# Token rows kept in one buffer of twelve from load to store, second operand copies, and a new order of steps, in a four-layer attention kernel

## What is computed

```python
# L0, and L3 with other weights: cross attention to ctx, residual
Q = x @ Wq + bq;  K = ctx @ Wk + bk;  V = ctx @ Wv + bv
x = x + softmax(Q @ K.T / 16) @ V @ Wo + bo
# L1: layer norms, attention to ctx ("a") and to side ("v"), then a layer norm and a dense layer ("fc")
t = attend_a(ln(x), ln(ctx)) + attend_v(ln(x), ln(side)) + x
x = ln(t) @ fc_W + fc_b + t
# L2: attention whose softmax runs over the query axis, layer norm with gain and bias
w = softmax((x @ Wq + bq) @ (ctx @ Wk + bk).T / 16, over x's tokens)
x = ln(w @ (ctx @ Wv + bv) + x) * gamma + beta
```

## Time and profile before

| | us |
|---|---|
| median of 3 runs | 557.83 |
| lowest and highest run | 557.55, 558.46 |
| span of the profiled execution, first to last instruction | 557.1 |
| PE busy | 545.8 (98%) |
| DVE busy | 478.4 (86%) |
| POOL busy | 480.7 (86%) |
| ACT busy | 447.2 (80%) |
| transfers of q1, share of 16 engines | 43.0% |

### The profile page before, as it was taken

One profiled execution on the slowest core, in us unless ns is written; L12 is line 12 of the kernel. 1 busy time (PEld: TensorE's weight loads), 2 busy tenths in 40 slices (PEclk: granted clock), 3 DMA queues, 4 the chain that ended last, 5 costly groups with the idle time before them and its releaser, 6 DMA issues.

```text
span 557.1 us, 16210 instructions
## 1 busy us (share of the span) xinstructions
PE 545.8 (98%) x4492; PEld 534.9 (96%) x4492; DVE 478.4 (86%) x1472; ACT 447.2 (80%) x1568; POOL 480.7 (86%) x672
## 2 busy tenths in 40 slices
PE   8999999999999999999999999999999999999995
PEld 7999999999999999989999999999999999999994
DVE  2588799888999889989897997999898987998884
ACT  2799987889778797869879798877888979798663
POOL 4999997999988989979997899977999998766793
PEclk9999999999999999999999999999999999999999
DMA  8993472344553345453247263453433432221112
GB/s 238 352 326 126 118 215 90 121 147 149 172 168 111 113 143 152 149 174 124 80 139 202 67 190 102 145 172 122 139 122 115 124 105 78 77 96 58 39 40 95
DMA packets 74440, 76.58 MB, mean 137 GB/s; under 512 B 7664, under 2 KB 58224, under 8 KB 74352
## 3 DMA queue, kind: packets, MB, share of 16 engines
q1 hardware_dynamic: 74352, 75.55, 43.0%
HBM read 50.87 MB, written 24.64 MB: 136 GB/s over the span
## 4 chain that ended last, share of the span: by engine, by line
PE 87%; POOL 4%; DMA 3%; issue 2%; DVE 2%; SPq 1%; ACT 1%; DVEq 0%; POOLq 0%; ACTq 0%
PE bank L793 15%; PE bank L806 10%; PE bank L800 9%; PE bank L776 7%; PE bank L817 5%; PE bank L819 5%; PE bank L818 5%; PE bank L949 5%; PE bank L927 5%; PE bank L784 5%; PE bank L830 4%; PE bank L902 3%; PE bank L903 3%; PE bank L904 3%; DMA side_in<-in_side 1%
## 5 line engine op out<-in xcount | busy, mean ns | idle before, releaser
L1065 ACT ACTIVATE prob_L<-bank,neg_max_L 128x128 f32<-128x128 f32 x320 | 114.5, 375 | 15.7 <-DVE neg_max_L L1376 13.6
L1065 ACT ACTIVATION_READ_ACCUMULATOR prob_L<-bank,neg_max_L 128x1 f32 x320 | 68.3, 214 | 0.0
L1376 DVE TENSOR_REDUCE neg_max_L<-bank 128x2 f32<-128x256 f32 (+1 forms) x128 | 60.5, 479 | 7.1 <-PE bank L800 4.3
L1546 POOL TENSOR_TENSOR rstd_ln<-var_eps_ln,minus_half 128x2 f32<-128x2 f32 x64 | 45.2, 707 | 18.5 <-ACT var_eps_ln L1078 18.2
L994 ACT ACTIVATE oT_hi_L<-bank 128x256 fp32r<-128x256 f32 (+1 forms) x96 | 44.4, 471 | 12.4 <-PE bank L806 11.1
L1219 DVE TENSOR_TENSOR oT_lo_L<-bank,oT_hi_L 128x256 fp32r<-128x256 f32 (+1 forms) x96 | 47.2, 501 | 5.6 <-ACT oT_hi_L L994 4.9
L994 ACT ACTIVATE probT_L<-bank 128x256 f32<-128x256 f32 (+1 forms) x96 | 44.4, 470 | 9.0 <-PE bank L784 8.6
L1333 DVE BATCH_NORM_STATS2 stats_ln<-x 128x6 f32<-128x256 f32 x128 | 47.5, 413 | 0.2
L1219 DVE TENSOR_TENSOR xT_lo_L<-bank,xT_hi_L 128x512 fp32r<-128x512 f32 x64 | 43.1, 677 | 3.7 <-ACT xT_hi_L L994 3.5
L1611 POOL TENSOR_TENSOR x_bias<-x,bias_fc 128x512 f32<-128x512 f32 x32 | 41.1, 1285 | 5.8 <-DVE x L1409 5.8
L1588 POOL TENSOR_TENSOR xT_lo_L<-x_in,xT_hi_L 128x512 fp32r<-128x512 f32 x32 | 41.2, 1286 | 5.4 <-ACT xT_hi_L L994 5.4
...
## 6 DMA issues: line engine op xcount, KB each, us to landing
...
keysT<-keys_out SPq DMA_DIRECT2D x128, 64.0 KB, 2.0
...
```

What stands on the lines that cost most here:

```text
L1065: last = activation(at(prob[k], g)[:, b, :], block(bank, b), ACT.Exp, bias=at(neg_max[k], g)[:, b:b + 1], accum_out=at(total[k], g)[:, b:b ...
L1376: dve.tensor_reduce(at(neg_max[k], g)[:], scores, AX.X, ALU.max, negate=True).then_inc(done[f"max_{k}"], 1)
L1546: pool.tensor_tensor(at(rstd[k], g)[:], at(var_eps[k], g)[:], minus_half[:, 0:n], ALU.pow).then_inc(done[f"rstd_{k}"], 1)
```

## The change

- The eleven kinds of row buffers are replaced by one, `x`, with 12 copies. load_x fills it, and every step of POOL and DVE named above reads and writes it in place until `store` sends it. The transposed half of the input goes into a buffer of its own, `xT_in` (3 copies), by an issue of its own, `load_xT`. `xhat` (2) remains for the norm of L1.
- Waits follow from that. load_x of group g waits for x_bias of g-4 and from group 12 on for the landing of the store of g-12. store waits for the store of g-4, load_ctx for hi_ctx of g-4. On POOL, x1_bias waits for norm_ln1 (it waited for out_L0), x2_bias for T_fc and stats_lnf (it waited for out_L1), x_res for T_L3 besides norm_ln2. On DVE, out_L2 waits for turn_x3. The waits for free copies of x1, x2, x3, x4, y and the biases fall away.
- Copies that go from 1 to 2: xT_hi and xT_lo of L1, fc and L3, qT_L1, oT_hi and oT_lo of L1 and L3, prob_L2, keys_turned, x3_turned. x3T goes from 2 to 3. ctx_in (10), side_in (3), keys (3), B2 (6), V2 (3) and the others stay.
- STARTS, PREPARATIONS and SEATS are new for every step. At the start SP's order is now cols, x of groups 0 to 3, ctx 0, xT 0, ctx 1, side 0 and 1, the weights Wq and Wk of L0, those of L2, xT 1, ctx 2, xT 2, side 2, the L2 value weights, ctx 3, xT 3, side 3, fc, send_keys 0, ctx 4, Wq and Wk of L1v, Wv and Wo of L0, side 4. It was cols, the Wq and Wk of L2, side 0, ctx 0, Wv and Wo of L0, Wq and Wk of L1v, two rows, x 0, Wq and Wk of L0. A weight pair Wq, Wk is 384 KB, a side 128 KB, each other load 256 KB.
- The two rows of the tables on which the x3 trip rests, and the head of the new PREPARATIONS:

```diff
-    "send_x3": [6717, 7506, 8500, 9484, 11385, 14234, 15144, 16085, 17392, 18944, 22232, 22803, 23951, 25582, 27885, 28913,
-        31460, 32548, 34537, 36189, 37379, 38161, 39750, 41584, 43944, 45995, 47291, 48508, 50317, 50950, None, None],
+    "send_x3": [7912, 8317, 9083, 11118, 11947, 12352, 14490, 16834, 17277, 20546, 20641, 21136, 24157, 26620, 27034, 30042, 30772,
+        32689, 33895, 34525, 37635, 38082, 40538, 43436, 44397, 46167, 48138, 48200, 49600, 50563, None, None],
...
-    "S_L2": [7443, 8333, 9249, 10165, 12349, 15646, 16594, 17648, 18883, 19792, 23354, 24714, 24918, 26289, 29338, 29676, 32154,
-        33443, 35753, 37572, 38166, 39128, 40499, 42359, 44749, 46974, 48398, 49596, 51139, 51646, 51999, 52772],
+    "S_L2": [8570, 8989, 9728, 11809, 12592, 12954, 15333, 17487, 17905, 21344, 21433, 21813, 24752, 27341, 27774, 30694, 31375,
+        33347, 34644, 35257, 38226, 38702, 41178, 44181, 45010, 46821, 48832, 48922, 50345, 51195, 51329, 51988],
...
+PREPARATIONS = {"first_constant": 0, "load_cols": 1, "constants": 14, "run_up": 26, "rep_fc": 278, "rep_L0": 326, "load_qk_L0": 447,
+    "load_qk_L2": 580, "scaled": 752, "M_L0": 812, "load_v_L2": 857, "M_L2": 911, "M_hi_L0": 931, "M_lo_L0": 973,
+    "load_fc": 1120, "M_hi_L2": 1123, "rep_L3": 1143, "k_L2": 1169, "M_lo_L2": 1233, "Wv2_hi": 1249, "load_qk_L1v": 1312,
+    "k_bias2": 1398, "m_L0": 1413, "load_vo_L0": 1414, "m_col_L0": 1524, "n_fc": 1533, "Wv2_lo": 1551,
...```

The code of SP, and three of the steps in place (the others are like them):

```diff
             def load_x(g):
-                earlier(sp, "x_bias", g, len(x_in))
-                earlier(sp, "lo_L0", g, len(x_in))
-                sp.dma_start(at(x_in, g)[:].rearrange("p a n -> p (a n)"), ins["x"][g]).then_inc(at(landed["x"], g), 16)
+                earlier(sp, "x_bias", g, IN_FLIGHT)
+                if g >= len(x):
+                    before = g - len(x)
+                    sp.wait_ge(at(stored, before), 16 * (before // IN_FLIGHT + 1))
+                sp.dma_start(flat(at(x, g)), ins["x"][g, :, 0:GROUP * D]).then_inc(at(x_landed, g), 16)
+
+            def load_xT(g):
+                earlier(sp, "lo_L0", g, len(xT_in))
+                sp.dma_start(at(xT_in, g)[:], ins["x"][g, :, GROUP * D:]).then_inc(at(landed["xT"], g), 16)
 
             def load_ctx(g):
+                earlier(sp, "hi_ctx", g, IN_FLIGHT)
                 earlier(sp, "O_L3", g, len(ctx_in))
-                sp.dma_start(at(ctx_in, g)[:].rearrange("p a n -> p (a n)"), ins["ctx"][g]).then_inc(at(landed["ctx"], g), 16)
+                sp.dma_start(at(ctx_in, g)[:].rearrange("p a n -> p (a n)"), ins["ctx"][g]).then_inc(at(ctx_landed, g), 16)
 
             def load_side(g):
...
             def store(g):
                 sp.wait_ge(done["out_L3"], g + 1)
-                sp.dma_start(out[g * GROUP:(g + 1) * GROUP].rearrange("b p e -> p b e"), at(y, g)[:]).then_inc(at(stored, g), 16)
+                if g >= IN_FLIGHT:
+                    sp.wait_ge(at(stored, g), 16 * (g // IN_FLIGHT))
+                sp.dma_start(out[g * GROUP:(g + 1) * GROUP].rearrange("b p e -> p b e"), at(x, g)[:]).then_inc(at(stored, g), 16)
...
             def out_L2(g):
                 dve.wait_ge(done["out_fc"], g + 1)
+                if g < LATE:
+                    dve.wait_ge(done["turn_x3"], g + 1)
                 dve.wait_ge(done["OUT_L2"], g + 1)
-                earlier(dve, "norm_ln2", g, len(x4))
-                plus("out_L2", g, "OUT_L2", x3, x4)
+                plus("out_L2", g, "OUT_L2")
...
             def x2_bias_of(g):
...
-                pool.wait_ge(done["out_L1"], g + 1)
-                earlier(pool, "out_fc", g, len(x2_bias))
-                pool.tensor_tensor(at(x2_bias, g)[:], at(x2, g)[:], every(bias["fc"]), ALU.add).then_inc(done["x2_bias"], 1)
+                pool.wait_ge(done["T_fc"], g + 1)
+                pool.wait_ge(done["stats_lnf"], g + 1)
+                pool.tensor_tensor(at(x, g)[:], at(x, g)[:], every(bias["fc"]), ALU.add).then_inc(done["x2_bias"], 1)
```

More of the change, by code:

```diff
@@ L268 @@
+    "n_fc": [7],
+    "mean_fc": [3],
[11 rows of a table added]
     "M_L1a": [0],
[3 rows of a table removed]
[3 rows of a table added]
     "m_L1a": [3],
[5 rows of a table removed]
[L278 to L279 removed]
[10 rows of a table removed]
[L290 to L293 removed]
[5 rows of a table removed]
[L299 to L302 removed]
[5 rows of a table added]
@@ new lines @@
+    "T_fc": [7, 4, 5, 5, 7, 6, 1, 5, 5, 4, 3, 7, 1, 0, 2, 7, 5, 1, 3, 0, 5, 2, 5, 1, 1, 0, 3, 7, 2, 5, 6, 0],
+    "OUT_fc": [0, 6, 5, 0, 5, 2, 5, 4, 5, 6, 0, 2, 5, 1, 4, 0, 1, 5, 1, 7, 0, 5, 6, 2, 5, 0, 1, 7, 6, 0, 3, 2],
[9 rows of a table added]
+}
+COPIES = {"ctx_in": 10, "side_in": 3, "keys": 3, "keysT": 2, "B2": 6, "xT_hi_L0": 1, "xT_lo_L0": 1, "prob_L0": 1, "neg_max_L0": 2,
[4 rows of a table added]
+    "stats_keys": 2, "mean_var_keys": 2, "var_eps_keys": 2, "rstd_keys": 2, "stats_ln1": 2, "mean_var_ln1": 2, "var_eps_ln1": 2,
+    "rstd_ln1": 2, "stats_lnf": 2, "mean_var_lnf": 2, "var_eps_lnf": 2, "rstd_lnf": 2, "stats_ln2": 2, "mean_var_ln2": 2,
+    "var_eps_ln2": 2, "rstd_ln2": 2, "ctxT_hi": 2, "ctxT_lo": 1, "shift_ln2": 2, "V2": 3, "keys_turned": 2, "x3_turned": 2,
+    "x3T": 3, "less_mean_ln2": 2, "xhat": 2, "x": 12, "xT_in": 3}
@@ L1414, in out_L0 @@
                 dve.wait_ge(done["OUT_L0"], g + 1)
[L1415 to L1417 removed]
+                scaled_plus("out_L0", g, "OUT_L0", inv_total["L0"])
             def out_L1(g):
@@ L1421, in out_L1 @@
                 dve.wait_ge(done["OUT_L1"], g + 1)
-                earlier(dve, "x2_bias", g, len(x2))
-                earlier(dve, "T_fc", g, len(x2))
-                plus("out_L1", g, "OUT_L1", x1_bias, x2)
+                plus("out_L1", g, "OUT_L1")
             def out_fc(g):
@@ L1429, in out_fc @@
                 dve.wait_ge(done["OUT_fc"], g + 1)
-                earlier(dve, "turn_x3", g, len(x3))
-                earlier(dve, "out_L2", g, len(x3))
-                scaled_plus("out_fc", g, "OUT_fc", rstd["lnf"], x2_bias, x3)
+                scaled_plus("out_fc", g, "OUT_fc", rstd["lnf"])
             def v_L2(g):
```

201 lines of the change are left out of this document (89 added, 112 removed), and 410 rows, old and new, of tables (COPIES, PREPARATIONS, SEATS, STARTS).

## The result

The changed kernel takes 588.88 us (median of four runs, 586.77 to 591.02) beside 558.14 for the kernel before on the same chips: a ratio of 1.0537, with a 95% interval of 1.0472 to 1.0603. The sign was the one that got most of the chance. The time lies 23 us above the upper end of the range, and above all rivals.

What follows compares the result with a forecast made beforehand. PE's fixed work bounds the kernel, so only its lag counts: span 557.1 + 3.7 (start) + 2.5 (middle) - 3.1 (run-out) = 560.2, and 560.9 us as the median lies 0.7 above. Range for eight in ten: 555.3 to 565.5.

Steps and rivals of the forecast that it cites:

- The sign: Whole kernel: slower than before, chance 0.62, against 0.15 for the same and 0.23 for faster.
- the range: Whole kernel: 555.3 to 565.5 us, meant to hold eight in ten.
- all rivals: Whole kernel: order runs as due, 555.1 us (0.23); effects cancel, 557.8 (0.15); ring of x holds SP, 566 (0.12).
- What bounds it, the work: PE: 532.6 us of work in any order, instructions unchanged; only PE's lag can be won or lost.
- the run-out: From T_L2 of group 31 to the last OUT_L3: idle PE falls to 1.2 us, -3.1 us.
- In place costs nothing: POOL additions on x: updating in place takes no longer, 1285 ns against 1287 from another buffer.
- The start: Up to O_L0 of group 1: weights land late and PE runs at half rate, +3.7 us (2.2 to 5.0).
- The sum for M_L0: First product at the start: 2.51 MB moved from 2.9 us on at 360 GB/s puts it at 9.9 us.
- the bound at 278 GB/s, 11.9: First product at the start: the same 2.51 MB at the slower rate put it at 11.9 us.
- The x3 trip: Middle: x3's way through DRAM before S_L2 overruns its allowance, 6.6 us of PE holes (2 to 9.8).
- What else there is: 2.0: Middle: holes from all other engines late by tenths, 2.0 us (1 to 4).
- The ring of x holds SP: Rival (c): load_x waits for stores, delaying SP's queue 0.2 to 0.4 in each of 20 groups, 566 us; chance 0.12.

Runs made afterwards that it cites:

- e15: The kernel before, own buffers and waits, with x1_bias, x2_bias and x_res moved later on POOL as the in-place update forces: 565.2 us, ratio 1.012.
- e2: The changed kernel with six landing semaphores for ctx in place of four: 585.0 us, ratio 1.049.
- e3: The changed kernel with the first four loads of x issued behind the ctx load of group 5: 590.5 us, ratio 1.059.
- e8: The changed kernel with six ctx semaphores, first x loads later, and fetch_x3 reading what group g-2 wrote (doesn't compute the function): 579.9 us, ratio 1.039.
- e6: The changed kernel with six ctx semaphores, first x loads later, eleven ctx_in copies and ctx loads from group 10 on earlier: 574.2 us, ratio 1.031.
- e9: The kernel before with ctx loads from group 10 on issued no earlier than 2.85 us ahead of their first reader: 565.8 us, ratio 1.015.
- e7: The changed kernel with six ctx semaphores, first x loads later, thirteen x and eleven ctx_in copies, their loads earlier: 572.4 us, ratio 1.026.
- e5: The changed kernel with six ctx semaphores, first x loads later and a thirteenth copy of x: 577.2 us, ratio 1.034.

## Why the prediction was wrong

**What bounds it, the work, the run-out.** Right. PE's work is unchanged and every microsecond of the loss is lag of PE. The run-out gave 2.5 us for 3.1 forecast.

**In place costs nothing.** Right for the durations. Wrong as a statement on the order: e15 shows 7 us for additions that may only start once their row was read, in an order made without this. In the new order POOL's waits of this kind are 8.0 us in all; no run shows what they cost there.

**The start: +3.7 forecast, +16.2 measured.** Three steps failed. (1) The sum for M_L0 took a load as landed when its last byte could have been moved. M_L0 was put at 9.9 and came at 12.3. The bytes were nearly right: the 2.51 MB up to the end of WkT of L0 had been moved by 10.3 us (244 GB/s on average). But the load landed only 1.9 later. In e2, with the same issues ahead of it, the bytes were there by 10.5 and the load at 11.9; in e3, with 1.46 MB to its end, by 7.2 and at 8.2. So 1.0 to 1.4 us from the last byte to the landing are missing from the sum. In the changed kernel a late part adds to them: the trace tells a landing by sixteen events, and of the 32 of Wq and Wk of L0 thirty had come by 11.1, the last at 12.24. Why it was late is open. It is not what was issued behind, for all loads of the first 12 us landed in the order of their issue. That the bound at 278 GB/s, 11.9, was nearer is luck: the rate wasn't what failed. (2) The wait of load_ctx for hi_ctx of g-4 was told in the description and priced nowhere. I had asked of each new wait whether it is due in time (0.45 us to spare), and not what stands behind it in SP's queue once PE is late. e2 prices it at 5.6 us of lag at Q_L1 of group 3. (3) I stopped at O_L0 of group 1, at 31 us by the old order. The preparations go on to 57 us in the new one, and 7 of the 16.2 arose behind that point (19.4 at O_L0 of group 1 and 27.4 at Q_L1 of group 3, for 10.2 and 11.2 before). The 9.2 us that no edit removed are a mis-sized term whose cause isn't settled.

**The x3 trip: 6.6 us of holes forecast, 8.0 measured in 11 places.** Right in place, size and number, but it was a small part of the loss: e8 took a leg of the trip away, 2.1 us of the holes went, and 1.3 us of the time. A hole that one wait makes shelters the others, and this I had even used to shrink the estimate, but not to ask what else stood there.

**"What else there is: 2.0".** This is the step that failed most. It stood for every other wait of the middle, taken from what the old order had left over. In the trace of before all loads but side_in are early, so no row there prices a late ctx or x. The tables did: the median reserve of ctx fell from 12.3 to 3.3 us, and that of x from 37.4 to 5.8, against a transfer of 2.8 (ctx, kernel before). I had computed such reserves for the x3 trip only, because the trace showed holes there. e6 (-6.9 us) and e9 (+8 us) show from both sides that ctx's reserve was a part of it, the largest that any run found. The 5.6 us that the middle of e7 has over that of the kernel before are open; its holes before S_L2 are 5.3 us.

**The ring of x holds SP.** It was rival (c) at 0.12, with 4 to 8 us. The wait came true: 33.7 us of SP's time in 16 places, longest 3.9, where 0.2 to 0.4 each were forecast. I had used 2.3, the landing at the median, as if half of the stores weren't slower and as if SP's other work didn't wait meanwhile. What it cost is less sure: 4 us by e5's median, 0.5 in the middle by its lags.

**The range.** All cases priced one cause at a time and let the rest run as due. What the runs point to is that they feed each other: a late engine frees a buffer late, SP stands at it, loads behind it come late, and an engine that works in order stands at them. No term of the sum has that. The hole before OUT_L0 of group 20 shows it once, and the edits' gains, which don't add up, fit it.
